# A recurrence whose projected inputs are seeded into PSUM by VectorE, and a projection taken straight from the residual

## The chip, the cores and the metric

The kernel runs on one core of one Trainium2 chip. The metric is the device time of one execution in microseconds. Three runs of the kernel before took 256.16, 258.83 and 258.78 us; the median is 258.78.

## The reference, cut to what matters

Three stages follow each other on an array of 32 batches x 32 channels x 400 positions (16 x 25), all fp32. A small graph convolution block comes first. Then, for each batch, an attention over the 400 positions with weights `softmax(exp(-dist2))`, added to its input. Then the part that the change is about:

```
x  = ln(residual, over channels)              # layer norm without weights
Wx = x @ W.T
Wx = (Wx - mean) * rsqrt(var + eps) * gamma + beta    # mean, var per channel over all batches and positions
y_t = sigmoid(Wx_t + y_{t-1} @ V.T)           # a scan over the 400 positions
out = residual + y
```

The scan is a contraction, so the kernel doesn't run it over 400 steps. It cuts the positions into 40 chunks of 10 and runs all chunks side by side: a first sweep of 10 steps from zero, then a second sweep of 10 steps in which each chunk starts from the end of the chunk ahead of it in the sweep before. The last values of both sweeps are compared; only where they differ would more sweeps be run, which these inputs don't need.

## The kernel before, in words

**Layout.** A group `g` is 4 batches x 32 channels = 128 partitions, 400 columns; there are `G` = 8 groups. The weights of channel operations are block diagonal 128 x 128 matrices in `cst`. PSUM is `ps`, 8 banks of 512 fp32 columns. `t0` holds the residual of all groups. Each engine has an instruction list of its own, written out by hand in the order of execution; engines are tied together only by semaphores that count finished pieces of work. So the order of the lists is the whole schedule: an instruction that waits holds up all that stands behind it on its engine.

**Attention.** Per group the scores are 13 tiles, in `UNITS` = 7 units of two tiles (the last has one). For unit `u`, TensorE runs `scores` (L918 to L933), ScalarE `inner` (L457, PSUM to SBUF) and one unit later `outer` (L464, in place), VectorE `add_tiles` (L671). `scores` of a unit may only start when `inner` of the unit two before it is done, since there are two pairs of banks. The work of the group before is put between the units: on TensorE `products` behind units 1, 2, 4 and 5, `sums` and `tail_sums` behind unit 3 (L935 to L964); on VectorE the reciprocal (L680) behind unit 2, quotient and residual addition (L687, L691) behind unit 4.

**Layer norm and projection of a finished group**, two to three groups behind the scores: `center2` (L970, behind unit 4 of the scores of group g+2) subtracts the channel mean by a matmul, ScalarE squares (L470), `variance2` (L976, behind unit 6) averages, ScalarE takes Ln and Exp for the inverse root (L475, L478, behind units 0 and 1 of group g+3), VectorE multiplies the centered values by it into `xl2` (L695), `wx` (L980) projects with `wT`, and VectorE takes batch statistics of that (L701). Banks 6 and 7 serve this (`NORM_BANKS`); the last groups use others. `variance2` waits for the statistics of an earlier group, which free its bank.

**Batch norm.** When all 8 groups have statistics, VectorE, TensorE and ScalarE work out mean, variance, scale and shift (L742 to L757) by operations on a column or two. The scale is then folded into the projection weight: `diag`, a matmul with `w` (L1034), a copy to `wsc` (L760). ScalarE loads the sigmoid table meanwhile (L523).

**Recurrence.** The 8 groups are two halves `h` of 4, 160 columns each. For step `s` TensorE runs two matmuls of `wsc` with `xl2` (L1045, one a half), then two of `vT` with the last `y` (L1050), which add to them; ScalarE takes the sigmoid with the shift as bias into `yb` (L533). The loop body holds 5 steps. In the second sweep VectorE adds each finished step to the residual (L778). Then SyncE stores `outs` in four transfers (L302), and the comparison of the sweeps runs beside that.

Of the kernel before, what the change touches and what calls it, by code (L numbers as in the profile page):

```python
# [26 lines left out]
ALU = mybir.AluOpType  # L27
# [3 lines left out]
N = T * V  # L31
NB = 4
G = B // NB
# [10 lines left out]
UNROLL = 5  # L44
BANKS = (0, 1, 2, 3, 1)
# [34 lines left out]
def build(nc, x_tok, x, consts, out):  # L80
    with ExitStack() as ctx:
# [17 lines left out]
        xl2 = sb("xl2", [P, G, N])  # L99
# [8 lines left out]
        wsc = sb("wsc", [P, P])  # L108
        diag = sb("diag", [P, P])
# [49 lines left out]
        def col(n, w=1, rows=P):  # L159
# [5 lines left out]
        mv, mm, tot, m2, vv, lnv, rsv, scl, msc, shf, okc = (  # L165
            col(25, 2), col(27, 2), col(29, 2), *(col(n) for n in range(31, 39)))
# [24 lines left out]
        centered2, sq2_ready, var2_done, ln2_ready, rs2_ready, xl2_ready, wx_done, stat_ready = (  # L191
            sem(n) for n in ("centered2", "sq2_ready", "var2_done", "ln2_ready", "rs2_ready", "xl2_ready",
                             "wx_done", "stat_ready"))
        bn_c, bn_pe, bn_act, wsc_ready, start_ok, cmp_c, cmp_pe, flag_ok, added = (
            sem(n) for n in ("bn_c", "bn_pe", "bn_act", "wsc_ready", "start_ok", "cmp_c", "cmp_pe", "flag_ok",
                             "added"))
# [7 lines left out]
        OUT_G = 2  # L204

# [7 lines left out]
        LAST_BANKS = {G - 3: NORM_BANKS, G - 2: (6, 1), G - 1: (2, 3)}  # L213
# [29 lines left out]
        def _(sp):  # L243
# [55 lines left out]
            def store_output(sums):  # L299
                sp.wait_ge(added, L * sums)  # L300
                for g in range(0, G, OUT_G):
                    sp.dma_start(out[g:g + OUT_G].rearrange("g p n -> p g n"),  # L302
                                 outs[:, g:g + OUT_G, :]).then_inc(out_done, 16)
                sp.wait_ge(out_done, 16 * (G // OUT_G) * sums)
# [58 lines left out]
        def _(act):  # L363
# [102 lines left out]
            def norm2(g, step, banks=NORM_BANKS):  # L466
# [4 lines left out]
                elif step == 1:  # L471
                    act.wait_ge(var2_done, g + 1)
                    if banks[0] != NORM_BANKS[0]:
                        act.wait_ge(xl2_ready, g + CREDIT1)
                    nc.scalar.activation(rs2, ps[:, banks[1], 0:N], ACT.Ln, bias=c_("eps")).then_inc(ln2_ready, 1)  # L475
# [4 lines left out]
            def weights(g, par):  # L480
# [3 lines left out]
                for u in range(UNITS):  # L484
# [21 lines left out]
            for g in range(1, 4):  # L506
                weights(g, g % 2)
            with act.Fori(2, PAIRS) as i:
                for par in range(2):
                    weights(2 * i + par, par)  # L510
            outer(G - 1, 1, UNITS - 1)
            for step in range(1, 3):
                norm2(G - 3, step)
            for g in (G - 2, G - 1):
                for step in range(3):
                    norm2(g, step, LAST_BANKS[g])
            act.wait_ge(bn_c, 4)
            nc.scalar.activation(lnv, vv, ACT.Ln, bias=c_("eps")).then_inc(bn_act, 1)
# [5 lines left out]
            act.wait_ge(wsc_ready, 1)  # L524
            act.wait_ge(bn_c, 8)

            def steps(base, count):
                with act.Fori(0, count // UNROLL) as i:
                    for k, bank in enumerate(BANKS):
                        s = UNROLL * i + k  # L530
                        for h in range(2):
                            act.wait_ge(pre[h], base + s + 1)
                            nc.scalar.activation(  # L533
                                yb[:, bass.ds(s + 1, 1), 4 * h:4 * h + 4, :].rearrange("p o g c -> p (o g c)"),
                                ps[:, 4 * h + bank, 0:HALF], ACT.Sigmoid, bias=shf).then_inc(y_ok[h], 1)
# [628 lines left out]
```

## Time and profile before

| | |
|---|---|
| Median of 3 runs | 258.78 us (256.16 to 258.83) |
| Profiled execution: span, first to last instruction | 256.3 us (the page gives no other time of it) |
| Busy: TensorE, VectorE, ScalarE, GpSimd | 208.7 (81%), 151.3 (59%), 170.7 (67%), 27.5 us (11%) |
| Mean granted TensorE clock | 0.944 of full speed |
| L1045, 80 instructions / L1050, 80 | 16.3 us busy / 17.1 us busy |
| Additions to the residual, L778, 10 | 0.737 us each |
| Load of the sigmoid table, L523 | 1.28 us, from 216.10 |
| HBM read, written | 14.74 MB, 11.88 MB |

An fp32 matmul shows as two instructions in the counts above, and its busy times overlap where matmuls follow closely. A granted clock of 1.00 is 2.4 GHz, 0.50 is 1.2 GHz. "Idle before" names the time in which an engine stood still ahead of an instruction and what released it.

### The profile page before, as it was taken

Reading aid. Unit: us, or ns where it says so; the run is one execution under the profiler, and the core shown is the slowest. Engines: PE = TensorE matmul, PEld = TensorE weight load, DVE = VectorE, ACT = ScalarE, POOL = GpSimd, SP = SyncE. Lnnn points to the kernel's source line nnn. Section 1 sums busy time; section 2 is a strip of 40 time slices with the busy share of each in tenths; the row PEclk is TensorE's granted clock in tenths of the full one; section 3 lists DMA queues with packets and bytes.
Section 4 is the critical chain, followed back from the end, with each engine's and each line's share of the span. In section 5 each row is a group of like instructions: output and inputs, shape, how many; then the busy total and the mean of one; then the engine's idle time right before and its main releaser. Section 6 shows DMA issues by size and latency. Waiting matters only on the chain.

```text
span 256.3 us, 4008 instructions
## 1 busy us (share of the span) xinstructions
PE 208.7 (81%) x1186; PEld 106.6 (42%) x1186; DVE 151.3 (59%) x284; ACT 170.7 (67%) x307; POOL 27.5 (11%) x44
## 2 busy tenths in 40 slices
PE   0395998998998979598999899999995944998950
PEld 0272653643643535123334333334332211987850
DVE  0147639929929915959667777777776544001560
ACT  2127398599499598979899898989894222254540
POOL 6000000260140050521010100001000000000000
PEclk9997999999999999979999999999998895599996
DMA  6910010096994091786451606070000000000006
GB/s 246 299 45 27 14 54 0 8 314 197 295 306 136 30 330 42 255 267 173 97 163 35 192 2 182 18 194 1 0 0 0 0 0 0 3 0 0 0 8 251
DMA packets 26881, 26.81 MB, mean 105 GB/s; under 512 B 1550, under 2 KB 25806, under 8 KB 26740
## 3 DMA queue, kind: packets, MB, share of 16 engines
q1 hardware_dynamic: 26724, 25.51, 33.8%
q10 hardware_dynamic: 144, 1.13, 1.3%
q8 instruction: 7, 0.11, 0.2%
q14 instruction: 6, 0.05, 0.1%
HBM read 14.74 MB, written 11.88 MB: 104 GB/s over the span
## 4 chain that ended last, share of the span: by engine, by line
PE 39%; DVE 21%; ACT 19%; issue 9%; DMA 6%; SPq 3%; DVEq 0%; ACTq 0%
DVE arena L680 6%; ACT arena L457 5%; PE ps L1045 5%; PE ps L1050 5%; DVE arena L598 5%; ACT arena L464 5%; PE ps L930 4%; PE ps L856 3%; DMA cst<-consts 3%; PE ps L832 3%; SPq L261 2%; ACT arena L389 2%; PE ps L842 2%; PE ps L868 2%; PE ps L976 2%
## 5 line engine op out<-in xcount | busy, mean ns | idle before, releaser
L457 ACT ACTIVATE arena<-ps 128x800 f32<-128x800 f32 (+1 forms) x56 | 44.4, 795 | 8.1 <-PE ps L930 6.4
L464 ACT ACTIVATE arena<-arena 128x800 f32<-128x800 f32 (+1 forms) x56 | 46.3, 828 | 0.0
L930 PE MATMUL ps<-qa,ka 128*128 128x400 bf16 (+1 forms) x128 | 35.4, 340 | 3.2 <-ACT arena L457 2.9
L930 PE MATMUL ps<-qb,kb 96*128 96x400 bf16 (+1 forms) x128 | 35.3, 338 | 0.0
L671 DVE TENSOR_TENSOR psum<-arena 128x400 f32<-128x400 f32 x32 | 19.6, 611 | 14.7 <-ACT arena L464 14.7
L533 ACT ACTIVATE yb<-ps,small 128x160 f32 x40 | 13.8, 391 | 16.5 <-PE ps L1050 16.2
L671 DVE TENSOR_TENSOR psum<-psum,arena 128x400 f32<-128x400 f32 x32 | 19.5, 609 | 7.1 <-ACT arena L464 6.0
L963 PE MATMUL ps<-arena,vb 128*32 128x400 f32 x192 | 21.8, 530 | 1.2 <-issue 1.2
L680 DVE RECIPROCAL arena<-ps 128x400 f32<-128x400 f32 x8 | 21.2, 2651 | 1.3 <-PE ps L947 1.3
L930 PEld LDWEIGHTS ps<-qa,ka 128*128 128x128 bf16 (+1 forms) x128 | 10.4, 97 | 27.6 <-ACT arena L457 11.8
L856 PE MATMUL ps<-arena,cst 128*128 128x400 f32 x32 | 14.6, 584 | 6.5 <-DVE arena L598 6.5
L1045 PE MATMUL ps<-xl,wsc 128*128 x80 | 16.3, 331 | 2.2 <-DVE yb L766 1.2
L598 DVE COPY arena<-arena 32x400 f32<-32x400 f32 x48 | 17.2, 358 | 0.9
L1050 PE MATMUL ps<-yb,cst 128*128 x80 | 17.1, 340 | 0.0
L1045 PEld LDWEIGHTS ps<-xl,wsc 128*128 128x128 f32 x80 | 13.4, 211 | 3.2 <-issue 3.2
L616 DVE TENSOR_TENSOR arena<-ps,arena 128x400 f32<-128x400 f32 x8 | 4.2, 569 | 17.2 <-ACT arena L417 17.2
L930 PEld LDWEIGHTS ps<-qb,kb 96*128 96x128 bf16 (+1 forms) x128 | 10.4, 98 | 8.9 <-issue 4.9
L331 POOL TENSOR_TENSOR arena<-arena,cst 128x400 bf16<-128x400 f32 x4 | 4.6, 1146 | 86.6 <-ACT arena L436 86.6
L1050 PEld LDWEIGHTS ps<-yb,cst 128*128 128x128 f32 x80 | 13.2, 209 | 1.2
L402 ACT ACTIVATE t<-arena,small 128x400 f32 (+1 forms) x8 | 4.8, 629 | 12.7 <-DVE arena L608 12.7
L856 PEld LDWEIGHTS ps<-arena,cst 128*128 128x128 f32 x32 | 5.5, 202 | 15.2 <-DVE arena L598 14.5
L778 DVE TENSOR_TENSOR outs<-t,yb x10 | 7.4, 737 | 6.8 <-ACT yb L533 6.8
(138 smaller groups left out, 358.8 us busy)
## 6 DMA issues: line engine op xcount, KB each, us to landing
dka<-arena SPq DMA_DIRECT2D x16, 200.0 KB, 3.0
dqa<-arena SPq DMA_DIRECT2D x16, 200.0 KB, 3.1
ka<-dka SPq DMA_DIRECT2D x8, 400.0 KB
qa<-dqa SPq DMA_DIRECT2D x8, 400.0 KB
arena<-x_tok SPq DMA_DIRECT2D x4, 400.0 KB
t<-x SPq DMA_DIRECT2D x1, 1600.0 KB, 12.6
dkb<-arena SPq DMA_DIRECT2D x8, 200.0 KB, 3.3
dqb<-arena SPq DMA_DIRECT2D x8, 200.0 KB, 4.3
```

The source lines that it names most:

```text
L457: nc.scalar.activation(prob[par][:, lo:hi, :], ps[:, o:o + hi - lo, 0:N], ACT.Exp, scale=2.0).then_inc(e1_done, 1)
L464: nc.scalar.activation(p, p, ACT.Exp).then_inc(p_ready, 1)
L533: nc.scalar.activation(yb[:, bass.ds(s + 1, 1), 4 * h:4 * h + 4, :].rearrange("p o g c -> p (o g c)"), ps[:, 4 * h + bank, 0:HALF], ACT.Si ...
L598: last = nc.vector.tensor_copy(*tap_input(par, j, k))
L671: nc.vector.tensor_tensor(dst, a, prob[par][:, t, :], ALU.add).then_inc(part_sum, 1)
L680: nc.vector.reciprocal(rden, ps[:, 5, 0:N]).then_inc(rden_ready, 1)
L832: last = mm_(ps[NB * CH * h:NB * CH * (h + 1), 2 * par, MT * tt:MT * tt + MT], xk[par][0:MT, o:o + NB * CH], mlo[:, h, :], start=True, sto ...
L856: mm_(ps[:, 2 * par + 1, 0:N], cst[:, o + P * j:o + P * j + P], tap_in[par][j], start=(j == 0), stop=False)
L930: last = mm_(ps[row:row + keys, bank, 0:N], kk[par][0:rows, b, o:o + keys], qq[par][0:rows, b, :], start=first, stop=not first, skip_group ...
L963: mm_(ps[C * b:C * b + C, 4, 0:N], vb[:, par, P * k + C * b:P * k + C * b + C], prob[par][:, FULL * b + k, :], start=(k == 0), stop=False, ...
L1045: mm_(ps[:, 4 * h + bank, 0:HALF], wsc[:, :], xl2[:, 4 * h:4 * h + 4, bass.ds(NC * s, NC)], start=True, stop=False)
L1050: mm_(ps[:, 4 * h + bank, 0:HALF], c_("vT"), yb[:, bass.ds(s, 1), 4 * h:4 * h + 4, :].rearrange("p o g c -> p (o g c)"), start=False, stop ...
```

## The change

1. **Projection straight from the residual.** Since centering and projecting are both matrices, their product `wc` = center x `wT` is made once, early (one matmul, one copy). For a group, `center2` now runs two matmuls of `t0`: one with `center` into bank 6, which only the variance needs, and one with `wc` into bank 7. `variance2` writes bank 6 again. VectorE's `project2` multiplies bank 7 by the inverse root into `ul`, which is kept in SBUF ordered by half and step; `stats` reads it there. `wx` and `norm2` on VectorE are gone.
2. **Places in the lists.** TensorE: `center2(g-2)` behind unit 0, `variance2(g-2)` behind the sums of unit 3. ScalarE: square, Ln, Exp of group g-2 behind units 1, 4, 5. VectorE: `project2(g-2)` and `stats(g-2)` at the end of the group's list. The second matmul of `center2(g)` waits for `u2_ready`, that is for `project2(g-1)`. The loop over the groups is written out.
3. **Batch norm.** Scale and negative shift by fewer, fused operations; `diag`, `wsc` and their matmul and copy are gone.
4. **Recurrence.** Steps have fixed slots in PSUM (three to a bank, step 0 in a bank of its own). Once, 8 bf16 matmuls of 480 columns write all slots (`prime`). Then VectorE writes `scl * ul - nshf` into the slots of a block of steps (`seed`), and the recurrent matmul adds to it (`start=False`). Step 0 of the first sweep has no matmul. Each half has its own start of the second sweep, and seeds for it are written as soon as a block has been read.
5. **Output.** The last step's addition is done by halves, and each half's two transfers wait only for their own.

```diff
 # TensorE
             def center2(g, banks=NORM_BANKS):
                 pe.wait_ge(t1_ready, g + 1)
-                if banks[0] == NORM_BANKS[0]:
-                    pe.wait_ge(xl2_ready, g + 1)
-                mm_(ps[:, banks[0], 0:N], c_("center"), at(t0, g), start=True, stop=True).then_inc(centered2, 1)
+                if g > 0:
+                    pe.wait_ge(ln2_ready, g)
+                mm_(ps[:, banks[0], 0:N], c_("center"), t0[:, g, :], start=True, stop=True).then_inc(centered2, 1)
+                if g > 0:
+                    pe.wait_ge(u2_ready, g)
+                mm_(ps[:, banks[1], 0:N], wc[:, :], t0[:, g, :], start=True, stop=True)
             def variance2(g, banks=NORM_BANKS):
                 pe.wait_ge(sq2_ready, g + 1)
-                if banks[1] == NORM_BANKS[1]:
-                    pe.wait_ge(stat_ready, g + 1)
-                mm_(ps[:, banks[1], 0:N], c_("mean"), sq2, start=True, stop=True).then_inc(var2_done, 1)
+                mm_(ps[:, banks[0], 0:N], c_("mean"), sq2, start=True, stop=True).then_inc(var2_done, 1)
...
                     scores(g, par, u)
                     if since > 0 and u in PRODUCTS_AT:
                         products(g - 1, 1 - par, PRODUCTS_AT.index(u), first=since == 1)
+                    if since > 1 and u == 0:
+                        center2(g - 2)
                     if since > 0 and u == 3:
                         sums(g - 1, 1 - par, first=since == 1)
                         tail_sums(g - 1, 1 - par)
-                    if since > 1 and u == 4:
-                        center2(g - 2)
-                    if since > 2 and u == 5:
-                        wx(g - 3)
-                    if since > 1 and u == 6:
-                        variance2(g - 2)
+                        if since > 1:
+                            variance2(g - 2)
...
+            def prime(bank):
+                mm_(ps[:, bank, 0:PRIMED], ka[0][:, 0, 0:P], ka[0][:, 0:2, :].rearrange("p b n -> p (b n)")[:, 0:PRIMED],
+                    start=True, stop=True).then_inc(primed, 1)
...
+            def step(h, s):
+                mm_(step_slot(h, s), c_("vT"), y_half(h, s), start=False, stop=True,
+                    skip_group_check=True).then_inc(pre[h], 1)
+            def steps(sweep):
+                for s in range(L):
+                    for h in range(2):
+                        pe.wait_ge(seeded[h], len(BLOCKS) * sweep + block_of(s) + 1)
+                        if s == 0:
+                            pe.wait_ge(start_ok[h], sweep)
+                        else:
+                            pe.wait_ge(y_ok[h], L * sweep + s)
+                        step(h, s)
 # ScalarE
-                    if u in (0, 1) and since > 2:
-                        norm2(g - 3, u + 1)
-                    if u == 4 and since > 1:
-                        norm2(g - 2, 0)
+                    if u in (1, 4, 5) and since > 1:
+                        norm2(g - 2, (1, 4, 5).index(u))
...
+            def step(h, s):
+                nc.scalar.activation(y_half(h, s + 1), step_slot(h, s), ACT.Sigmoid).then_inc(y_ok[h], 1)
 # VectorE
+            def project2(g, banks=NORM_BANKS):
                 dve.wait_ge(rs2_ready, g + 1)
-                nc.vector.tensor_tensor(at(xl2, g).rearrange("p (s c) -> p s c", s=L),
-                                        ps[:, banks[0], 0:N].rearrange("p (c s) -> p s c", s=L),
-                                        rs2.rearrange("p (c s) -> p s c", s=L), ALU.mult).then_inc(xl2_ready, 1)
+                nc.vector.tensor_tensor(ul[:, g // 4, :, g % 4, :],
+                                        ps[:, banks[1], 0:N].rearrange("p (c s) -> p s c", s=L),
+                                        rs2.rearrange("p (c s) -> p s c", s=L), ALU.mult).then_inc(u2_ready, 1)
...
                 for u in range(UNITS - 1):
                     add_tiles(g, par, u)
-                    if since > 2 and u == 0:
-                        norm2(g - 3)
...
                     if since > 0 and u == 4:
                         quotient(g - 1, first=since == 1)
                         residual(g - 1)
+                if since > 1:
+                    project2(g - 2)
+                    stats(g - 2)
...
+            def seed(h, n):
+                lo, hi = BLOCKS[n]                  # BLOCKS = ((0, 1), (1, 4), (4, 7), (7, 10))
+                bank = 4 * h + (3, 0, 1, 2)[n]
+                nc.vector.tensor_scalar(ps[:, bank, 0:SLOT * (hi - lo)],
+                                        ul[:, h, lo:hi, :, :].rearrange("p s g c -> p (s g c)"),
+                                        scl, nshf, ALU.mult, ALU.subtract).then_inc(seeded[h], 1)
...
+            for n in range(len(BLOCKS)):
+                for h in range(2):
+                    dve.wait_ge(primed, 1 + PRIME_ORDER.index(4 * h + (3, 0, 1, 2)[n]))
+                    seed(h, n)
+            for n in range(len(BLOCKS) - 1):
+                for h in range(2):
+                    dve.wait_ge(y_ok[h], BLOCKS[n][1])
+                    seed(h, n)
+            for h in range(2):
+                chain(h, L)
             nc.vector.tensor_copy(ys, yb[:, L, :, :]).then_inc(cmp_c, 1)
+            for h in range(2):
+                seed(h, len(BLOCKS) - 1)
 # SyncE
-                sp.wait_ge(added, L * sums)
-                for g in range(0, G, OUT_G):
+                for h in range(2):
+                    sp.wait_ge(added, LAST_STEP_ADDS * (sums - 1) + L + h)
+                    for g in range(4 * h, 4 * h + 4, OUT_G):
```

## Rows read from the trace of the kernel before

**Rows 1.** The page, part 4: the chain of waits, share of the span by engine.

```profile
PE 39%; DVE 21%; ACT 19%; issue 9%; DMA 6%; SPq 3%; DVEq 0%; ACTq 0%
```

**Rows 2.** Timeline (start, us, instruction), windows (length, busy by engine, clock), chain: attention.

```profile
131.42 0.84 ACT L457 ACTIVATE arena<-ps 128x800 f32<-128x800 f32 x1
...
144.04:156.66 12.62, 12.02 (x76) 4.58 (x75) 9.29 (x14) 11.37 (x17) 0.92 (x2) 1.00 0.33 85
...
181.91 0.04 ACT arena L457
```

**Rows 3.** Timeline, the tail from the last reciprocal to the first sigmoid.

```profile
201.95 2.66 DVE L680 RECIPROCAL arena<-ps 128x400 f32<-128x400 f32 x1 [1.28 <-PE ps L947]
...
206.43 0.94 PE L970 MATMUL ps<-t,cst 128*128 128x400 f32 x2 [0.15 <-DVE t L691]
...
211.04 1.70 PE L980 MATMUL ps<-xl,cst 128*128 128x400 f32 x2 [2.14 <-DVE xl L695]
...
213.40 0.37 DVE L742 BATCH_NORM_AGGREGATE small<-stat 128x2 f32<-128x48 f32 x1
...
220.36 0.92 ACT L533 ACTIVATE yb<-ps,small 128x160 f32 x2 [2.98 <-PE ps L1050]
```

**Rows 4.** Timeline and windows of the recurrence.

```profile
221.00:224.30 3.30, 3.30 (x15) 3.30 (x14) 0.00 (x0) 1.08 (x3) 0.00 (x0) 0.50 0.02 5
...
229.69 0.68 ACT L533 ACTIVATE yb<-ps,small 128x160 f32 x2 [0.52 <-PE ps L1050]
...
247.04 0.68 ACT L533 ACTIVATE yb<-ps,small 128x160 f32 x2 [0.53 <-PE ps L1050]
```

**Rows 5.** Timeline, SyncE: the issues of the output.

```profile
248.79 2.59 SPq L302 DMA_DIRECT2D out<-outs  x4
```

**Rows 6.** Timeline of group 5 into 6, TensorE (and one row of ScalarE).

```profile
167.66 0.91 PE L976 MATMUL ps<-sq,cst 128*128 128x400 f32 x2 [0.60 <-DVE stat L701]
...
168.41 0.33 PE L930 MATMUL ps<-qa,ka 128*128 128x400 bf16 x1
...
169.29 0.84 ACT L457 ACTIVATE arena<-ps 128x800 f32<-128x800 f32 x1 [0.91 <-PE ps L930]
...
170.68 0.34 PE L930 MATMUL ps<-qa,ka 128*128 128x400 bf16 x1
...
174.65 0.33 PE L930 MATMUL ps<-qa,ka 128*128 128x400 bf16 x1
...
177.01 0.33 PE L930 MATMUL ps<-qa,ka 128*128 128x400 bf16 x1
```

**Rows 7.** Timeline of the same stretch, ScalarE.

```profile
167.12 0.51 ACT L457 ACTIVATE arena<-ps 128x400 f32<-128x400 f32 x1 [0.25 <-PE ps L930]
...
167.52 0.86 ACT L464 ACTIVATE arena<-arena 128x800 f32<-128x800 f32 x1
...
170.93 0.84 ACT L457 ACTIVATE arena<-ps 128x800 f32<-128x800 f32 x1
...
172.83 0.84 ACT L457 ACTIVATE arena<-ps 128x800 f32<-128x800 f32 x1
```

**Rows 8.** Timeline, end of group 7: VectorE's last addition, its product, TensorE behind it.

```profile
195.56 0.58 DVE L671 TENSOR_TENSOR psum<-psum,arena 128x400 f32<-128x400 f32 x1
...
196.05 0.85 DVE L695 TENSOR_TENSOR xl<-ps,prep 128x400 f32<-128x400 f32 x1
...
197.04 1.67 PE L970 MATMUL ps<-t,cst 128*128 128x400 f32 x2 [1.74 <-DVE xl L695]
```

**Rows 9.** Timeline of two pauses of TensorE, and windows behind pauses (clock: third from last).

```profile
94.57 0.60 PE L880 MATMUL ps<-arena,prep 128*128 128x400 f32 x1 [1.70 <-DVE arena L616]
...
106.39 0.33 PE L930 MATMUL ps<-qa,ka 128*128 128x400 bf16 x1 [2.69 <-ACT arena L457]
...
108.40:111.60 3.20, 3.20 (x16) 0.67 (x16) 3.06 (x5) 2.39 (x4) 1.90 (x2) 0.50 0.96 330
...
197.10:200.40 3.30, 3.30 (x8) 1.28 (x12) 0.32 (x1) 0.50 (x1) 0.00 (x0) 0.50 0.00 0
```

More of the change, by code:

```diff
@@ L505, in _ @@
                         outer(0, 0, u - 1)
-            for g in range(1, 4):
+            for g in range(1, G):
                 weights(g, g % 2)
-            with act.Fori(2, PAIRS) as i:
-                for par in range(2):
-                    weights(2 * i + par, par)
             outer(G - 1, 1, UNITS - 1)
[L512 to L518, printed above, removed]
+            for step in range(3):
+                norm2(G - 2, step)
+            for step in range(3):
+                norm2(G - 1, step, LAST_BANKS)
+            act.wait_ge(bn_c, 3)
+            nc.scalar.activation(lnv, nvar, ACT.Ln, bias=c_("eps"), scale=-1.0).then_inc(bn_act, 1)
             act.wait_ge(bn_act, 1)
@@ L904, in _ @@
             mix_c(0)
+            mm_(ps[:, 5, 0:P], c_("center"), c_("wT"), start=True, stop=True).then_inc(wc_done, 1)
             branches(0)
@@ L1008, in _ @@
             pe.wait_ge(es_ready, G + CREDIT)
-            for g in range(1, 4):
+            for g in range(1, G):
                 pe.wait_ge(operands_in[g % 2], 96 * (g // 2 + 1))
                 attend(g, g % 2)
-            with pe.Fori(2, PAIRS) as i:
-                for par in range(2):
-                    g = 2 * i + par
-                    pe.wait_ge(operands_in[par], 96 * i + 96)
-                    attend(g, par)
-            products(G - 1, 1, 0, False)
-            center2(G - 2, LAST_BANKS[G - 2])
@@ L1019, in _ @@
-            wx(G - 3)
+            for k in range(FULL):
+                products(G - 1, 1, k, False)
             sums(G - 1, 1, False)
             tail_sums(G - 1, 1)
-            variance2(G - 2, LAST_BANKS[G - 2])
-            for k in range(1, FULL + 1):
-                products(G - 1, 1, k, False)
-            wx(G - 2, LAST_BANKS[G - 2])
-            center2(G - 1, LAST_BANKS[G - 1])
-            variance2(G - 1, LAST_BANKS[G - 1])
-            wx(G - 1, LAST_BANKS[G - 1])
-            pe.wait_ge(bn_c, 3)
@@ L1054, in _ @@
-            for sweep in range(2):
-                steps(L * sweep, sweep, L)
-            pe.wait_ge(cmp_c, 6)
+            products(G - 1, 1, FULL, False)
+            center2(G - 2)
+            variance2(G - 2)
+            center2(G - 1, LAST_BANKS)
+            variance2(G - 1, LAST_BANKS)
+            def prime(bank):
+                mm_(ps[:, bank, 0:PRIMED], ka[0][:, 0, 0:P], ka[0][:, 0:2, :].rearrange("p b n -> p (b n)")[:, 0:PRIMED],
+                    start=True, stop=True).then_inc(primed, 1)
@@ L1057, in _ @@
+            for s in range(1, L):
+                for h in range(2):
+                    pe.wait_ge(seeded[h], block_of(s) + 1)
+                    pe.wait_ge(y_ok[h], s)
+                    step(h, s)
+            steps(1)
+            pe.wait_ge(cmp_c, 4)
             mm_(ps[0:1, 7, 0:1], okc, c_("ones")[:, 0:1], start=True, stop=True).then_inc(cmp_pe, 1)
```

215 lines of the change are left out of this document (102 added, 113 removed).

## The prediction

> **What bounds the kernel now.** I read the chain of waits first. It is spread: TensorE 39%, VectorE 21%, ScalarE 19%, no single engine [rows 1]. So the change has to be costed stage by stage: attention, the tail after it, the recurrence, the output.
>
> Attention: one group of four batches takes 12.62 us, with TensorE busy for 12.02 of it and ScalarE for 11.37 [rows 2]. TensorE is nearly the bound, and ScalarE has some 1.2 us of slack. The first inner exponential of group 3 starts at 131.42 and that of group 7 at 181.91, four groups later [rows 2].
>
> The tail: from the last reciprocal, 201.95, to the first sigmoid, 220.36, is 18.4 us of serial small work, partly at 1.2 GHz [rows 3]. The recurrence: first sigmoid 220.36 to the last one's end at about 247.7, 27.4 us for 20 steps [rows 3, 4]. It is bound by TensorE, four fp32 matmuls a step, and from 221.0 to 224.3 the granted clock is still 0.50 [rows 4]. The end: the first output issue at 248.79 is 7.5 us before the end of the span [rows 5].
>
> **Recurrence: what goes.** Each step loses its two input matmuls; two `vT` matmuls of 160 columns stay. TensorE then no longer binds: a half waits for matmul, sigmoid, matmul. The price of a lone fp32 matmul: 400 columns took 0.94 us at full clock and 1.70 at half [rows 3]. fp32 goes at four cycles a column here (0.67 and 1.33 us of those), so the fixed part is 0.27 and 0.37, and 160 columns cost 0.54 and 0.90. The sigmoid is 0.39 (two in 0.68, 0.29 apart) [rows 4], the two handovers some 0.09. A step: 1.02 us at full clock, 1.38 at half. The halves overlap, since each occupies TensorE for only 0.27 (0.53) and ScalarE for 0.29. From first to last sigmoid: 0.39 + 19 x 1.02 + 0.3 (the sweep's copy on VectorE) + 0.3 (second half) = 20.4 at full clock; at half 0.39 + 19 x 1.38 + 0.3 + 0.5 = 27.4, which is what it takes now. I add 0.5 for a start at half clock: 20.9.
>
> The seeds (16 VectorE passes, eight a sweep) are beside the chain: the first two, 160 columns, lie under the sigmoid table's load; of the others, 480 columns (0.6 to 0.7 us, from the 0.58 of a 400-column addition [rows 8]), the next two are done as the first sigmoids end, and each later one has three steps of time. In the second sweep VectorE starts 1.5 us late and then has one addition of 0.74 us (table above) per 1.02 us step, so it catches up. If the cover went, each late seed would cost under 0.7 us, and only once a block.
>
> **Tail.** Now 11.45 us go from the last reciprocal to the aggregate at 213.40 [rows 3]. After: reciprocal, quotient, residual 3.9 (the norm product that stood between is gone); center matmul, then the second matmul must wait for `project2` of group 6, 1.2; its columns 0.67, variance 0.94, Ln and Exp 1.2, product 0.9, statistics 0.65: 9.5. From the aggregate to the first sigmoid now 6.96 us; after it there are three small VectorE operations of 0.2 fewer up to the table load, and nothing behind the load (its 1.28 us, table above, outlasts scale, shift and the first seeds): 3.4. The 8 primes sit on TensorE beside this.
>
> **Output.** The last addition is split, so the first half's store may be issued 0.5 us after that half's last sigmoid, itself 0.3 before the last; the four issues and the transfer then take the same 7.5. So 7.7 us follow the last sigmoid, against 8.5.
>
> **Attention: what the new order costs.** This is the step I weigh most. The number of matmuls a group stays the same (`wc` for `wx`), but the places move. `center2` now stands behind the first scores of a group, and its second matmul waits for `u2_ready`, that is for `project2` of the group before. `project2` is at the very end of VectorE's list, behind the two additions that need ScalarE's outer exponential of unit 5. TensorE is in order, so scores 1 of the next group, and with them ScalarE's inner 1, queue behind that wait.
>
> One cycle, from the `wc` matmul back to itself. TensorE: `wc`, scores 1, product 2.36 (as scores, product, center from 174.65 to 177.01), scores, product, scores, sums, tail 3.97 (170.68 to 174.65), variance 0.75, scores 4 until inner 4 may start 0.88 [rows 6]: 7.96. ScalarE: inner 4, outer 3, Ln, inner 5 1.90; inner 5, outer 4, Exp, inner 6 1.90 (both as 170.93 to 172.83); outer 5 0.40 later, and it lasts 0.86 [rows 7]: 5.06. VectorE: two additions and the product, 0.05 + 0.60 + 0.49 + 0.86, and the hop 0.13 [rows 8]: 2.13. Together 15.2 us a group instead of 12.62. Check on it: inner 1 must start 3.77 us after outer 5 ends (2.13 + 0.76 + 0.88), ScalarE could start it after 1.04; that is 2.7 us of new idle time, and 1.3 more comes before inner 4, less the 1.2 to 1.5 of idle time that the group has now. The present wait of the variance matmul for the statistics, 0.6 us, is what the edit removes; this replaces it. A lower bound is 2.7 + 11.2 = 13.9 us, if the wait before inner 4 doesn't come.
>
> Group 2 has the new matmuls without the wait: some 1.3 us later. Groups 3 to 6: 4 x 15.2. Group 7: the reciprocal came 20.0 after its first inner; now inner 4 is at 10.2, outer 5 ends at 15.3, the three products (behind the quotient at 14.9), sums and tail end at 19.2. So the stall of group 7 is paid back there, by the half clock that TensorE had at 197 and by the projection that no longer stands ahead of the sums.
>
> **Clock.** The new pause on TensorE is 3.0 us a group, in two parts, 1.8 and 1.2, with only the center matmul between. What the rows show: a pause of 1.74 us before 197.04 and one of 2.69 before 106.39 were each followed by granted clock 0.50 over all of the stretch shown (197.10 to 200.40, 108.40 to 111.60), and one of 1.70 before 94.57 was not [rows 8, 9]. The 3.3 us after such a fall would here be TensorE work on the cycle: 1.7 us lost each. Five pauses, some four falls: 6.8; one more for the 2.2 us pause before the last products, at some 60%: 1.0. The bounds are 0 and five falls, one of them twice as long: 10.
>
> The Trainium skill (TensorE: Matmul & The Clock Gate, section Why this matters for your kernels) warns only of pauses longer than either of these two parts; by it the clock would stay up here and the sum be that of rival A. The 1.74 us pause of this trace speaks against it.
>
> **Sum.** 131.4 + 1.3 + 60.8 = 193.5; reciprocal 19.2: 212.7; aggregate 9.5: 222.2; first sigmoid 3.4: 225.6; recurrence 20.9: 246.5; end 7.7: 254.2; with the falls 262.0. The profiled execution's span is 256.3, which lies at the low end of the three runs (256.16; the median 258.78 is 2.5 higher). I leave the sum where it is.
>
> **Rivals.**
> A. The clock holds through the new pauses: 254.2 to 255.2. For it: 94.57, where a pause of 1.70 cost nothing. Against: the other two. Faster than the median by 1.4 to 1.8%: with up to one fall it ends at 256.9 at most, from two on it doesn't count as faster. This is the case on the other side. 22%.
> B. As forecast, but the clock is low in the whole recurrence. A step at half clock has TensorE occupied for 1.07 of 1.38 us. In the trace it began at 218.3 and was still at 0.50 from 221.00 to 224.30, busy all the time [rows 4], so a thinner load may never raise it; the primes (8 x 0.4 us at half clock) fill the time ahead, and if the clock falls behind them nothing as dense follows. +6.5: 268.5. 18%.
> C. The second matmul doesn't wait long, because `project2` is done earlier than the queue says: attention stays at 12.6 a group. Then inner 0 of group 7 is at 182, the last group 3.1 us shorter, the end near 240. The order of the three queues speaks against it; only a misread count of a semaphore would bring it. 7%. With the lower bound of 13.9 a group and no fall 247 to 249: 5%.
> D. The forecast, 258 to 266: 48%.
>
> **How the numbers follow.** About 1% (2.6 us round 258.78) is what a measurement of this kernel can tell from no change. Faster than 256.2: A (20 of its 22), C with its bound (12): 32%. Within: the low part of D and the rest of A: 20%. Slower than 261.4: the rest of D, and B: 48%. The range leaves out C and the top of B: 249 to 269. D's own is 258 to 266.
>
> **What would show it.** Right: first scores of groups 3 to 7 about 15.2 us apart or more; TensorE idle for 2 to 3 us before the `wc` matmul, released by the VectorE product into `ul`; ScalarE idle before each inner 1; granted clock 0.50 right behind these pauses; first sigmoid 3.4 us after the aggregate; steps of 1.0 to 1.1 us at full clock. Wrong: a period near 12.6 (then the time is near 240); a clock at 1.00 throughout attention (254 to 255); steps of 1.4 us in the recurrence (B); VectorE's seeds ahead of a step's matmul as its releaser (the cover is gone).

## The result: slower, and the profile after

Four executions of the changed kernel gave a median of 269.64 us (265.42 to 270.37), against 258.07 us (256.16 to 258.83) for the kernel before, now with a fourth execution: a ratio of 1.037, 95% interval 1.029 to 1.045. The ratios here and below compare only executions within 1.5% of the fastest of their kernel (of the changed kernel 265.42 and 269.39); the two medians stand at 1.045. The profiled execution took 269.39 us by the clock of the metric, of which its span is 267.5: 1.9 us lie outside the span.

The spans of both profiles, cut at the same events (the first inner exponential of a group, the sigmoids); the falls of the forecast in the third row are those of groups 3 to 7:

| us | before | after | forecast |
|---|---|---|---|
| start to the first inner of group 2 | 119.7 | 120.6 | 119.7 |
| group 2 | 11.7 | 16.7 | 13.0 |
| groups 3 to 6 | 50.5 | 68.0 | 60.8, and 6.8 of falls |
| group 7 and tail, to the first sigmoid | 38.5 | 33.0 | 32.1, and 1.0 |
| first sigmoid to the last one's end | 27.4 | 21.0 | 20.9 |
| last sigmoid to the end | 8.6 | 8.2 | 7.7 |

So groups 2 to 6 of attention became 22.5 us longer, and everything from group 7 on 12.3 us shorter. The 0.9 us ahead of group 2 lies within scatter: in the profiled execution of another kernel below, which differs from this one only from group 2 on, that stretch took 124.4 us.

First the chain of waits of the page, the line that answers to [rows 1]: TensorE's share has gone up, ScalarE's down.

```profile
PE 45%; DVE 24%; ACT 14%; issue 6%; DMA 5%; SPq 4%; DVEq 0%; ACTq 0%
```

The four groups 3 to 6, as windows (start:end and length, busy time of TensorE, weight loads, VectorE, ScalarE, GpSimd, granted clock, share and GB/s of the DMA engines). They answer to the window of [rows 2].

```profile
137.34:155.35 18.01, 15.32 (x74) 5.06 (x74) 9.34 (x14) 11.48 (x19) 1.13 (x2) 0.81 0.28 75
...
155.35:172.95 17.60, 15.29 (x74) 5.03 (x74) 9.34 (x14) 11.47 (x18) 1.13 (x2) 0.81 0.25 62
...
172.95:190.29 17.34, 15.41 (x74) 5.16 (x74) 9.34 (x14) 11.48 (x19) 1.13 (x2) 0.80 0.30 79
...
190.29:205.36 15.07, 12.38 (x74) 4.43 (x74) 9.33 (x14) 11.26 (x19) 1.30 (x2) 1.00 0.28 71
```

ScalarE does the same 11.3 to 11.5 us of work a group as before and now stands still for 3.8 to 6.5 us of each, where it was 1.25. Three groups have a mean clock of about 0.8; the fourth kept 1.00 and took 15.07 us. That is the 15.2 us of the forecast, and the other three are the same cycle with falls of the clock in it.

The cycle in the timeline, at the end of group 4's list and the start of group 5's (start, length, instruction, idle time before it and what ended it):

```profile
172.62 0.57 DVE L708 TENSOR_TENSOR t<-t,sq 128x400 f32<-128x400 f32 x1
...
173.25 1.70 PE L1003 MATMUL ps<-t,cst 128*128 128x400 f32 x2 [1.52 <-DVE t L708]
...
173.72 0.57 DVE L688 TENSOR_TENSOR psum<-psum,arena 128x400 f32<-128x400 f32 x1
...
174.21 0.85 DVE L712 TENSOR_TENSOR ul<-ps,prep 128x400 f32<-128x400 f32 x1
...
175.11 1.70 PE L1006 MATMUL ps<-t,wc 128*128 128x400 f32 x2 [0.16 <-DVE ul L712]
...
178.19 0.84 ACT L474 ACTIVATE arena<-ps 128x800 f32<-128x800 f32 x1 [3.96 <-PE ps L962]
...
185.27 0.84 ACT L474 ACTIVATE arena<-ps 128x800 f32<-128x800 f32 x1 [1.44 <-PE ps L962]
```

TensorE waits 1.52 us for the residual addition (L708), runs the center matmul at half clock, and then waits for the product (L712), which VectorE begins only behind the addition at 173.72. The scores that inner 1 needs are behind both, so ScalarE is idle for 3.96 us; at 185.27 it is idle for another 1.44, before inner 4. These are the two stalls of the forecast. Over the four groups the list of waits says the same:

```profile
ACT arena L474 <- PE ps L962: 22.3, 12, 4.0
...
PE ps L1003 <- DVE t L708: 6.1, 4, 1.5
```

The clock, again as windows, one within each of groups 3, 4 and 5:

```profile
139.10:145.70 6.60, 6.20 (x22) 1.94 (x26) 1.50 (x3) 2.18 (x4) 0.00 (x0) 0.50 0.31 65
...
156.20:162.80 6.60, 6.06 (x19) 1.75 (x18) 2.35 (x4) 2.41 (x4) 0.00 (x0) 0.50 0.44 105
...
173.20:179.90 6.70, 6.49 (x18) 1.96 (x19) 2.42 (x5) 2.74 (x5) 0.00 (x0) 0.50 0.59 160
```

In group 5 the fall began at the end of the pause's first part, in group 3 in its second, and it lasted well into the scores and products behind it. In group 4 it began in between, while the center matmul ran (155.65 to 156.97). So in groups 4 and 5 the clock fell before the second part of the pause had come; in groups 3 and 7 it fell in the second part. Group 2, where the forecast was short:

```profile
122.22 1.70 PE L1003 MATMUL ps<-t,cst 128*128 128x400 f32 x2 [1.79 <-DVE t L708]
...
126.09 0.84 ACT L474 ACTIVATE arena<-ps 128x800 f32<-128x800 f32 x1 [4.21 <-PE ps L962]
```

The first center matmul waits 1.79 us for the residual of group 0 and then runs at half clock; ScalarE stands still for 4.21 us before inner 1.

The tail, the recurrence and the output in the timeline, where [rows 3, 4, 5] stood before:

```profile
225.45 2.66 DVE L697 RECIPROCAL arena<-ps 128x400 f32<-128x400 f32 x1 [0.80 <-PE ps L979]
...
234.78 0.37 DVE L753 BATCH_NORM_AGGREGATE small<-stat 128x2 f32<-128x48 f32 x1
...
238.38 0.50 ACT L537 ACTIVATE yb<-ps 128x160 f32<-128x160 f32 x2
...
253.72 0.66 ACT L537 ACTIVATE yb<-ps 128x160 f32<-128x160 f32 x2 [0.33 <-PE ps L1065]
...
254.71 0.66 ACT L537 ACTIVATE yb<-ps 128x160 f32<-128x160 f32 x2 [0.33 <-PE ps L1065]
...
258.47 0.73 DVE L801 TENSOR_TENSOR outs<-t,yb 128x320 f32<-128x320 f32 x1 [0.27 <-ACT yb L537]
...
258.69 0.66 ACT L537 ACTIVATE yb<-ps 128x160 f32<-128x160 f32 x2 [0.33 <-PE ps L1065]
...
259.57 2.59 SPq L319 DMA_DIRECT2D out<-outs  x4
```

The window of the primes and first steps:

```profile
234.70:241.30 6.60, 5.84 (x17) 3.09 (x17) 5.41 (x15) 2.89 (x7) 0.00 (x0) 0.50 0.00 0
```

From the last reciprocal to the aggregate 9.33 us (forecast 9.5), from there to the first sigmoid 3.60 (3.4), a step at full clock 0.99 (1.02). The clock was at 0.50 while the primes and the first steps ran and then rose; rival B did not come. The output issue is at 259.57, only 0.2 us after the last sigmoid ends, but that is 0.6 after the first half's: VectorE was still at the addition of step 8 for both halves (258.47, 0.73 us long) when the first half's last sigmoid was done, at 258.99.

### The profile page after: what moved, and what is told of

It is laid out like the page before. It is cut to its first block, busy times and chain, and to the rows that moved or that the text cites. A ratio compares the mean times of both kernels' runs of the same rounds, so it can differ in the third digit from the quotient of the medians.

```text
span 267.5 us, 3545 instructions
## 1 busy us (share of the span) xinstructions
PE 211.5 (79%) x1110; PEld 96.0 (36%) x1110; DVE 160.6 (60%) x297; ACT 168.7 (63%) x307; POOL 28.8 (11%) x44
## 4 chain that ended last, share of the span: by engine, by line
PE 45%; DVE 24%; ACT 14%; issue 6%; DMA 5%; SPq 4%; DVEq 0%; ACTq 0%
PE ps L962 8%; DVE arena L613 6%; PE ps L995 5%; PE ps L1065 5%; ACT arena L481 4%; SPq L277 4%; PE ps L1006 4%; DMA cst<-consts 3%; PE ps L863 3%; ACT arena L474 3%; DVE psum L688 3%; PE ps L873 2%; DVE ps L772 2%; PE ps L979 2%; DMA dqb<-arena 2%
## 5 line engine op out<-in xcount | busy, mean ns | idle before, releaser
L962 PE MATMUL ps<-qa,ka 128*128 128x400 bf16 (+1 forms) x128 | 38.3, 363 | 4.3 <-ACT arena L474 3.9
L962 PE MATMUL ps<-qb,kb 96*128 96x400 bf16 (+1 forms) x128 | 37.6, 356 | 0.0
L995 PE MATMUL ps<-arena,vb 128*32 128x400 f32 x192 | 23.7, 576 | 2.0 <-DVE sq L704 2.0
L1065 PE MATMUL ps<-yb,cst 128*128 128x160 f32 x76 | 17.9, 354 | 2.0 <-DVE yb L779 0.3
L537 ACT ACTIVATE yb<-ps 128x160 f32<-128x160 f32 x40 | 12.1, 304 | 8.9 <-PE ps L1065 7.5
L1003 PE MATMUL ps<-t,cst 128*128 128x400 f32 x16 | 9.3, 672 | 10.6 <-DVE t L708 10.6
L1065 PEld LDWEIGHTS ps<-yb,cst 128*128 128x128 f32 x76 | 12.0, 199 | 8.3 <-issue 4.7
L358 POOL COPY vb<-vst 128x384 f32 (+1 forms) x8 | 5.4, 677 | 85.8 <-PE ps L991 85.8
L1006 PE MATMUL ps<-t,wc 128*128 128x400 f32 x16 | 11.1, 787 | 3.5 <-DVE ul L712 3.5
L419 ACT ACTIVATE t<-arena,small 128x400 f32 (+1 forms) x8 | 4.8, 629 | 12.4 <-DVE arena L623 12.3
L399 ACT ACTIVATE arena<-ps,small 128x400 f32<-128x400 f32 x8 | 5.4, 685 | 10.0 <-PE ps L873 9.8
```

The lines of the kernel that those rows point to most:

```text
L537: nc.scalar.activation(y_half(h, s + 1), step_slot(h, s), ACT.Sigmoid).then_inc(y_ok[h], 1)
L962: last = mm_(ps[row:row + keys, bank, 0:N], kk[par][0:rows, b, o:o + keys], qq[par][0:rows, b, :], start=first, stop=not first, skip_group ...
L995: mm_(ps[C * b:C * b + C, 4, 0:N], vb[:, par, P * k + C * b:P * k + C * b + C], prob[par][:, FULL * b + k, :], start=(k == 0), stop=False, ...
L1006: mm_(ps[:, banks[1], 0:N], wc[:, :], t0[:, g, :], start=True, stop=True)
L1065: mm_(step_slot(h, s), c_("vT"), y_half(h, s), start=False, stop=True, skip_group_check=True).then_inc(pre[h], 1)
```

## The experiments

The theories: **A**, the places of the new pieces in the lists make a group's cycle 15.1 us; what the clock adds comes on top. **B**, the clock is all of the loss. **C**, something else of the change slows attention, such as the written-out loop or statistics from SBUF.

### The old places with all the rest of the change

```diff
 # TensorE
-                    if since > 1 and u == 0:
-                        center2(g - 2)
...
-                        if since > 1:
-                            variance2(g - 2)
+                    if since > 1 and u == 4:
+                        center2(g - 2)
+                    if since > 1 and u == 6:
+                        variance2(g - 2)
 # ScalarE
-                    if u in (1, 4, 5) and since > 1:
-                        norm2(g - 2, (1, 4, 5).index(u))
+                    if u in (0, 1) and since > 2:
+                        norm2(g - 3, u + 1)
+                    if u == 4 and since > 1:
+                        norm2(g - 2, 0)
 # VectorE
+                    if since > 2 and u == 0:
+                        project2(g - 3)
...
+                    if since > 2 and u == 2:
+                        stats(g - 3)
...
-                if since > 1:
-                    project2(g - 2)
-                    stats(g - 2)
...
```

> The changed kernel with the layer norm's pieces back at the places of the kernel before: both matmuls of center2 behind unit 4, the variance behind unit 6, Ln and Exp behind units 0 and 1 of the next group, product and statistics on VectorE behind units 0 and 2. Projection from the residual, seeds, batch norm and output stay as changed. Theory A (the places make attention slow; a group took 15.1 us at full clock and 17.3 to 18.0 where the clock fell, against 12.6): a group takes 12.0 to 12.6 us, no pause of TensorE over 1 us between groups 3 and 7, and since the tail and the recurrence keep what they gained the time is about 241 us (238 to 246). Theory B (the clock alone, which falls because the list has more for TensorE to wait on anywhere): 250 to 258. Theory C (something else of the change slows attention: the written-out loop, statistics from SBUF, the strided product): a group stays at 15 us or more, 262 to 268.

Measured: 241.38 us (239.51 to 242.72), 0.933 times the kernel before, interval 0.926 to 0.941. Two groups of it, as windows:

```profile
145.78:157.92 12.14, 12.05 (x76) 4.61 (x75) 9.50 (x14) 11.28 (x17) 0.92 (x2) 1.00 0.39 101
...
157.92:170.05 12.13, 12.05 (x76) 4.61 (x75) 9.49 (x14) 11.27 (x18) 0.92 (x2) 1.00 0.43 106
```

and from its list of waits, over groups 4 to 6:

```profile
ACT arena L474 <- PE ps L969: 2.6, 3, 0.9
```

A group takes 12.13 us, TensorE is busy for 12.05 of it at clock 1.00, and ScalarE waits 2.6 us for scores in three groups. Theory C falls: with the same written-out loop, the same `wc` matmul and the same statistics from SBUF, attention is even 0.5 us a group faster than before. TensorE's idle time in a group went from 0.60 us to 0.08, and 0.60 was the wait of the variance for the statistics [rows 6], which the change removes; that the one is the other is read from the sizes, no run separates it. Theory B falls too, as far as it says that the change's lists must wait wherever the pieces stand.

### The pair of matmuls one unit later

```diff
-                    if since > 1 and u == 0:
+                    if since > 1 and u == 1:
                         center2(g - 2)
```

> The changed kernel with one move: center2 (both matmuls) stands behind unit 1's scores and products instead of behind unit 0's scores, so that scores 1 no longer queue behind the two waits. Nothing else moves. Theory A: product into ul ends 2.1 us after a group's first inner, TensorE comes to the second matmul about then, so its pause shrinks to under 1 us; one wait of ScalarE stays, before inner 4, since the work between scores 1 and 4 is the same: a group takes about 13.4 us, the clock doesn't fall, the time is about 252 us (248 to 256). Theory B: the clock falls as before, 262 or more. Theory C: no change, 268 to 270.

Measured: 251.19 us (249.56 to 252.97), 0.970, interval 0.964 to 0.976.

```profile
163.59:177.07 13.48, 12.37 (x76) 4.43 (x74) 9.34 (x14) 11.36 (x18) 1.13 (x2) 1.00 0.40 100
```

One changed digit gives back 3.5 us a group against the mean of 17.0: the clock stays up and the cycle is 13.48 us, against 13.4 expected.

### The same waits with the clock held up

`fill_w` and `fill_x` are the constants in `cst`, read as bf16; their products are overwritten unread.

```diff
             def center2(g, banks=NORM_BANKS):
-                pe.wait_ge(t1_ready, g + 1)
                 if g > 0:
                     pe.wait_ge(ln2_ready, g)
+                if g < G - 2:
+                    for _ in range(8):
+                        mm_(ps[:, banks[0], 0:N], fill_w, fill_x[:, 0:N], start=True, stop=True)
+                pe.wait_ge(t1_ready, g + 1)
                 mm_(ps[:, banks[0], 0:N], c_("center"), t0[:, g, :], start=True, stop=True).then_inc(centered2, 1)
+                if 0 < g < G - 2:
+                    pe.wait_ge(e1_done, UNITS * (g + 2))
+                    for _ in range(4):
+                        mm_(ps[:, 2 * slot((g + 2) % 2, 1), 0:N], fill_w, fill_x[:, 0:N], start=True, stop=True)
                 if g > 0:
                     pe.wait_ge(u2_ready, g)
```

> The changed kernel, same places, same waits, but TensorE runs bf16 matmuls without use in both pauses of center2 of groups 0 to 5: 8 of 400 columns ahead of the wait for the residual (into bank 6), 4 ahead of the wait for the product (into banks of the next scores). They are extra work of about 2.1 us a group that fits in the pauses. Theory A: the clock stays at 1.00 through attention, every group takes 15.1 us as the one did whose clock had not fallen, about 7.7 us come back in groups 3 to 6 and some 1 us in group 2: about 260 us (257 to 263). Theory B (the clock is all of the loss): with the clock held a group takes 12.6 to 13 us and the time is 247 to 252. If the fillers themselves stood in the way of the next matmul, a group would take over 15.5 us at clock 1.00.

Measured: 260.34 us (257.51 to 262.96), 1.006, interval 1.001 to 1.012.

```profile
136.47:151.54 15.07, 14.41 (x87) 5.60 (x86) 9.33 (x14) 11.25 (x18) 1.29 (x2) 1.00 0.33 87
...
166.61:181.68 15.07, 14.42 (x87) 5.60 (x86) 9.34 (x14) 11.25 (x18) 1.28 (x2) 1.00 0.35 90
```

In its timeline, the two matmuls at the start of group 6:

```profile
181.98 0.94 PE L1009 MATMUL ps<-t,cst 128*128 128x400 f32 x2 [0.17 <-DVE t L708]
...
183.84 0.94 PE L1016 MATMUL ps<-t,wc 128*128 128x400 f32 x2 [0.25 <-DVE ul L712]
```

All four groups take 15.07 us, to a hundredth what the undisturbed group of the changed kernel took. TensorE's idle time ahead of the two matmuls shrinks to 0.17 and 0.25 us, filled with work of no use, and the cycle is the same: it is not TensorE's idleness that costs, it is when the residual and the product come. So the loss of groups 3 to 6 splits, against the kernel before: 4 x (15.07 - 12.62) = 9.8 us for the places, 7.7 us for the falls in the profiled execution (68.0 - 60.3). Against the first experiment, which has all the rest of the change, the places cost more, 60.3 - 48.4 = 11.9 us. By the medians the fillers give back 9.3 us, which includes group 2 (14.7 instead of 16.7, with the clock at 1.00).

### Only group 2

```diff
-                    if since > 1 and u == 0:
+                    if since > 1 and u == (1 if g == 2 else 0):
                         center2(g - 2)
```

> The changed kernel with center2 behind unit 1 only in the list of group 2 (where there is no wait for a product, only for the residual of group 0). Theory A: group 2 took 16.7 us from its first inner to that of group 3, where my forecast had 13.0; the residual of the group before is ready 1.5 us after TensorE asks for it, at half clock; with the move the wait is gone and group 2 takes about 13.5 us, so the time is about 3 us less, 266 to 267. Rival: group 2 is slow for its other new work (Ln, Exp, product, variance), and the time stays within 1 us.

Measured: 268.00 us (262.52 to 272.22), 1.022, interval 1.013 to 1.032.

```profile
124.40:137.73 13.33, 11.59 (x72) 4.24 (x70) 8.75 (x13) 11.36 (x19) 1.13 (x2) 1.00 0.39 104
```

Group 2 takes 13.33 us instead of 16.73, the 3.4 us expected. The median moved by only 1.6 us from 269.64, the ratio by 0.015, and the four executions scatter over 10 us, since the clock's falls in the later groups land elsewhere in each execution (groups 3 to 6 took 16.7, 15.1, 18.0 and 16.0 here). For the sum the experiment is inconclusive; for the cause of group 2 the window is clear.

### Only the second matmul one unit later

The two lines with # are a summary of the code, not its text.

```diff
 # in center2, for the groups of the loop, the matmul with wc is left out; then
+                    if since > 1 and u == 1:
+                        project_u(g - 2)              # wait for u2_ready, matmul with wc
 # VectorE, project2
+                dve.wait_ge(u_mm, g + 1)
```

> The changed kernel with only the second matmul of center2 (the one with wc) moved, behind unit 1's products; the first stays behind unit 0's scores and waits there for the residual of the group before. Theory A: TensorE's pause before the first matmul stays at some 1.5 us and the one before the second is gone; the work from there to scores 4 is as before, so a group takes about 13.9 us at full clock, 1.2 less than with both behind unit 0 and 0.5 more than with both behind unit 1 (13.5). The clock may still fall now and then (a pause of 1.5 us has done so in one case of three): 252 to 259, about 255. Rival (only the wait for the product counts, the one for the residual lies beside ScalarE's own work): a group takes 13.5 us, the time is 251.

Measured: 256.09 us (255.28 to 257.99), 0.998, interval 0.993 to 1.003. 

```profile
150.67:164.65 13.98, 12.21 (x74) 4.51 (x74) 9.34 (x14) 11.49 (x18) 1.13 (x2) 1.00 0.32 80
...
178.63:194.19 15.56, 13.78 (x74) 4.83 (x74) 9.35 (x14) 11.49 (x19) 1.14 (x2) 0.89 0.26 69
```

The two matmuls in its timeline:

```profile
164.95 0.94 PE L1005 MATMUL ps<-t,cst 128*128 128x400 f32 x2 [1.52 <-DVE t L709]
...
167.31 0.94 PE L1012 MATMUL ps<-t,wc 128*128 128x400 f32 x2
```

13.98 us at full clock, 13.9 expected, so the wait for the residual alone, 1.52 us, costs 0.5 us a group over the 13.48 with both behind unit 1, and the wait for the product the other 1.1. In one group of four the clock fell (mean 0.89) and the group took 1.6 us more: the price of one fall. Group 2 was again slow, 16.4 us, with the clock at 0.50 from 121.6 to 125.0.

### Only VectorE's product one place earlier

```diff
                     if since > 0 and u == 4:
                         quotient(g - 1, first=since == 1)
                         residual(g - 1)
+                    if since > 1 and u == 4:
+                        project2(g - 2)
                 if since > 1:
-                    project2(g - 2)
                     stats(g - 2)
```

> The changed kernel with one move on VectorE alone: project2 stands right behind the residual addition (behind unit 4), ahead of the two additions of unit 5; TensorE's and ScalarE's lists are as changed. Theory A (the cycle runs through VectorE's list end): the product ends 1.1 us earlier against the group's first inner, so a group whose clock didn't fall takes 14.0 us instead of 15.1, and TensorE's second pause is gone; the falls stay (the first pause alone is 1.5 us and more): 262 to 266. Rival (the product is released by the Exp or by TensorE, not by its place): a group at full clock stays at 15.1, the time at 269.

Measured: 256.87 us (254.00 to 258.52), 0.994, interval 0.989 to 0.999.

```profile
166.81:180.79 13.98, 12.22 (x74) 4.43 (x74) 9.25 (x14) 11.24 (x18) 1.29 (x2) 1.00 0.38 96
```

In its timeline, the product now beside the first matmul:

```profile
180.96 0.86 DVE L712 TENSOR_TENSOR ul<-ps,prep 128x400 f32<-128x400 f32 x1
...
181.09 0.94 PE L1004 MATMUL ps<-t,cst 128*128 128x400 f32 x2 [1.52 <-DVE t L708]
```

A group takes 13.98 us, so the two additions stood in the cycle with the 1.1 us that the forecast gave them. More could not come back: with TensorE's wait for the product gone altogether, in the experiment before, a group takes the same 13.98. My expectation for the whole, 262 to 266, was a miss: I expected the clock to go on falling behind the first pause, which is still 1.52 us. In groups 3 to 7 it fell once in this execution (group 7), and once in that of the experiment before (group 6), against four times in the changed kernel. With the product one place earlier the second part of the pause is gone, and fewer falls came; counts over all executions are at the end. Group 2 took 16.5 us here too; its clock was at 0.50 from 120.8, behind a wait of 2.23 us for the transfer into `qb`, ahead of the wait for the residual.

### The old kind of recurrence on the old places

```diff
-                seed(h, n)                            # VectorE, all blocks of both sweeps; and no primes
+            nc.vector.tensor_scalar(diag[:, :], c_("ident"), scl, None, ALU.mult).then_inc(seeded[0], 1)
...
+            def inputs(h, s, only=False):             # TensorE, ahead of each step's recurrent matmuls
+                ins = mm_(step_slot(h, s), diag[:, :], ul[:, h, s, :, :].rearrange("p g c -> p (g c)"),
+                          start=True, stop=only)
...
-                nc.scalar.activation(y_half(h, s + 1), step_slot(h, s), ACT.Sigmoid).then_inc(y_ok[h], 1)
+                nc.scalar.activation(y_half(h, s + 1), step_slot(h, s), ACT.Sigmoid, bias=shf).then_inc(y_ok[h], 1)
```

> Kernel e1_old_places with the old kind of recurrence: no primes and no seeds; each step has an input matmul a half again (a diagonal of the scale, made by VectorE, with the step's columns of ul; the shift is the sigmoid's bias), ahead of the recurrent one. Theory A (TensorE bound the recurrence with four matmuls a step; a lone chain of matmul and sigmoid takes 1.0 us): a step takes 1.07 to 1.2 us at full clock and 2.1 at half, where it was 0.99; first to last sigmoid 24 to 26 us instead of 20.5, the time about 246 us (244 to 249) against 241.4. Rival (steps are bound by the chain through ScalarE either way, and the seeds brought nothing but an earlier first sigmoid): within 1 us of e1_old_places.

Measured: 246.47 us (244.17 to 247.29), 0.955, interval 0.945 to 0.964; 5.1 us over the kernel with seeds and the same attention.

```profile
222.00:236.00 14.00, 14.00 (x103) 13.81 (x102) 6.02 (x11) 8.72 (x26) 0.00 (x0) 1.00 0.00 1
```

Two steps of it in the timeline:

```profile
234.03 0.68 ACT L542 ACTIVATE yb<-ps,small 128x160 f32<-128x160 f32 x2 [0.40 <-PE ps L1049]
...
235.12 0.68 ACT L542 ACTIVATE yb<-ps,small 128x160 f32<-128x160 f32 x2 [0.40 <-PE ps L1049]
```

and the window of the kernel with seeds on the same places:

```profile
213.00:231.00 18.00, 15.14 (x73) 10.53 (x72) 13.74 (x24) 10.86 (x36) 0.00 (x0) 1.00 0.00 1
```

With four matmuls a step TensorE is busy for all of 14.00 us and a step takes 1.09 (234.03 to 235.12); with two it is 0.99, and TensorE has idle time in each (15.14 of 18.00 busy, last window). From the first sigmoid to the last one's end: 23.7 us against 20.5, a little less than expected (24 to 26). The first two steps took 2.1 us each from sigmoid to sigmoid, against 1.65 and 1.00, which makes 1.6 of the 3.2 us; the 0.1 us in each later step makes the rest. The first sigmoid comes 4.1 us after the aggregate instead of 3.4. The rival, no gain from the seeds, falls. But not all of the 5.1 us between the medians need be the seeds: the profiled executions lie 5.9 us apart, and 2.3 of these arose ahead of group 2 (124.1 us against 121.8), where both kernels do the same.

The other 3.7 us of the kernel before's 27.4 no run separated. Its first two steps took 2.1 us as well; by its timeline 1.2 us lie at the change of sweep (2.57 us from sigmoid to sigmoid against 1.37), 0.8 at the two places where its loop starts anew (1.51 us), and 1.6 in its other steps, 1.2 us instead of 1.09.

## Why the prediction was right

The change was slower, as forecast, and for the two reasons that the forecast gave, a longer cycle and falls of the clock. The size was not met. The sum said 262.0, 3.2 us above the median of the kernel before; the median is 269.64, 11.6 us above its own. That lies outside the forecast's own 258 to 266 and 0.6 above the 269 of its whole range; only the ratio of 1.037, times 258.78, gives 268.3, inside it. The two terms that were mis-sized are group 2 and the step from span to time, both below. That 269.64 lies near rival B's 268.5 is chance: the low clock through the whole recurrence did not come.

**The cycle of attention.** Right, as the forecast had it: the period from the queue orders alone was 15.2 us, measured 15.07 wherever the clock held, in the changed kernel and in all four groups with fillers. Two of its parts were tested one by one, TensorE's place (13.48 when both matmuls come a unit later) and VectorE's last two additions (1.1 us); a third, the wait that ScalarE has before inner 4, was read from the trace (1.27 to 1.44, forecast 1.3). The lower bound of 13.9 did not apply.

**Falls of the clock.** Right in kind: four falls in five groups, as forecast, though that this execution had just four is a draw (see the last section). Their price was not: 6.8 us forecast for groups 3 to 7, 7.7 measured in groups 3 to 6 alone, for three falls. In these three groups the clock was low for 6.8 us each, where the forecast reckoned with 3.3, and they cost 2.3 to 2.9 instead of 1.7; that group 6 had no fall nearly made up for it. The fifth fall, for which the sum had 1.0 us, did not come: ahead of the last products TensorE stood still for 2.05 us before 221.65, and the clock was 1.00 from 210.7 to 234.5. Instead group 7 took 20.1 us to its last reciprocal, 0.9 more than forecast, with a fall of its own (207.3 to 210.7); what of it is the fall was not separated. Rival A did not come. By the rule of the Trainium skill that stood beside it (TensorE: Matmul & The Clock Gate, section Why this matters for your kernels) none of the pauses in groups 2 to 7, 1.8 us at the longest, was long enough; the traces speak against that.

**Group 2.** Mis-sized: 1.3 us forecast, 5.0 measured. The forecast gave it new matmuls "without the wait". It has no wait for a product, but the wait for the residual of group 0 was there as well, 1.79 us with a fall of the clock behind it. With both gone the group took 13.33 (1.6 over the kernel before), with the pauses filled and the clock up 14.68; so of the 3.4 us between 13.33 and 16.73 some 1.4 are the wait and 2.0 the fall.

**Tail and recurrence.** Right: 9.3 for 9.5, 3.6 for 3.4, 0.99 for 1.02 a step, 21.0 for 20.9 from first to last sigmoid. The seeds hid as forecast, but for the first pair of 480 columns: TensorE waited 0.73 us for a seed before the first recurrent matmul, a releaser that the forecast had named as a sign of being wrong, but only at the start. VectorE was busy with seeds without a break there, and the second pair of sigmoids came 1.7 us behind the first where 1.4 had been forecast at half clock.

**The end.** 0.5 us too low, but not by the split addition. It does queue behind the one for both halves of the step before, and still the issue came 0.2 us after the last sigmoid's end, as forecast. From the issue to the end of the span it took 7.9 us where 7.5 had been read from the kernel before; no run shows why.

**The sum.** 262.0 was forecast on the scale of the span, 267.5 measured: 3.7 of the 5.5 us are group 2, 0.9 came before it, 0.4 in groups 3 to 6, 0.5 at the end. The median lies 2.1 us higher still: 1.9 because I took the span for the time, 0.2 because the profiled execution was not the median. The difference is 1.9 us for the kernel before too (256.0 and 257.95 in one of its executions), so its 256.3 us of span did not lie at the low end of its times, and rival A's 254.2 to 255.2 would have read 256.1 to 257.1.

The version that beats both kernels is the first experiment's: all of the change, with the old places of the layer norm's pieces, 241.38 us.

## What to carry to other kernels

When work of an engine that is nearly full is moved in a hand-written list, ask at its new place what each wait is released by and what stands right behind it in the same list; pieces that cost no wait at their old places (12.1 us a group) made it 15.07 behind unit 0 with the clock up, because the release sat at the end of another engine's list and the next scores stood behind it. The period of such a cycle can be added up from start-to-start times of a trace to a per cent. And a gain in one stage (12 us from group 7 on) says nothing of a loss in another: the same change with the layer norm's pieces at their old places is 28 us faster.

## What the runs showed of the hardware that I had not expected

A pause of 1.5 us on TensorE between dense matmuls let the granted clock fall to 1.2 GHz in 2 of 10 groups (3 to 7 of the two kernels at 13.98 us), 0.7 to 0.8 us after the pause was over. The same pause, followed after one matmul by a second of up to 0.9 us, did so in 8 of 10 (groups 3 to 7 of the changed kernel and of the one with only group 2 altered). Three of these eight falls began before the second pause had come, as the first pause alone might have brought them; five began in the second or within 0.5 us behind it. So the second pause seems to bring most of them, on few cases. In three of the four groups of the changed kernel that had a fall the clock stayed low for 6.8 us, with TensorE busy for 6.3 to 6.5 us of them, in the fourth for 3.4. With the pauses filled it never fell in these groups.

Which groups fall changes from one execution to the next, and the time with it: the changed kernel took 265.42 us where its mean clock was 0.944, and 269.39 to 270.37 where it was 0.919 to 0.923; the one with group 2 altered took 262.5 to 272.2. The kernel without such pauses took 239.5 to 242.7.
